# Unread products of the identity in four places of TensorE's queue: a one-core attention and expert kernel

## The reference

```python
q = (layernorm(x) @ Wq + bq)          # (8, 512, 256), 16 heads of 16
k, v = ctx @ Wk + bk, ctx @ Wv + bv
attn = softmax(clip(q @ k.T * 16 ** -0.5, -1e4, 1e4))
x = x + tanh(g_xattn) * ((attn @ v) @ Wo + bo)

xn = layernorm(x)
logits = xn @ gate_weight.T                                # 8 per token
kth = sort(logits.reshape(-1))[4 * 256 * 6 - 1]
gates = logits * (logits >= kth)
h = gelu(xn @ w1[e].T + b1[e])                             # for each expert e
x = x + tanh(g_ffn) * sum_e(gates[..., e] * (h @ w2[e].T + b2[e]))
```

## Time and profile before

| | us |
|---|---|
| median of 3 runs | 2038.12 |
| lowest and highest | 2036.85, 2041.68 |
| the profiled execution | 2045.47 |
| its span, first to last instruction | 2043.7 |
| mean granted clock over the span | 0.968 of 2.4 GHz |

### The profile page before, as it was taken

The page is one execution under the profiler, slowest core; times in us unless marked ns, Lnnn a source line. Parts: engine busy times, 40 slices in busy tenths (PEclk is TensorE's granted clock), DMA queues, the critical chain, the costliest instruction groups (busy, mean ns, idle before and its releaser), DMA issues.

```text
span 2043.7 us, 31038 instructions
## 1 busy us (share of the span) xinstructions
PE 1917.6 (94%) x8916; PEld 1367.7 (67%) x8916; DVE 1339.5 (66%) x2333; ACT 1242.1 (61%) x2076; POOL 161.0 (8%) x334
## 2 busy tenths in 40 slices
PE   7899999999966989999999999999999999999998
PEld 5733333333335767788878878878877887887886
DVE  6688888888617886655755656565565566656555
ACT  4447676776632232576666767676666666767664
POOL 4201011101115440000000000000000000000000
PEclk9969999999968999999999999999999999999999
DMA  7932222222101325224222233322423223332221
GB/s 243 331 106 80 82 74 74 70 78 66 38 31 44 134 102 189 103 84 171 97 104 104 98 120 130 109 104 83 156 109 109 104 83 129 135 109 83 103 103 52
DMA packets 97267, 220.83 MB, mean 108 GB/s; under 512 B 31330, under 2 KB 49508, under 8 KB 87908
## 3 DMA queue, kind: packets, MB, share of 16 engines
q1 hardware_dynamic: 97124, 219.12, 31.2%
HBM read 178.57 MB, written 40.24 MB: 107 GB/s over the span
## 4 chain that ended last, share of the span: by engine, by line
PE 61%; DVE 4%; issue 2%; ACT 1%; POOL 1%; DMA 0%; SPq 0%; DVEq 0%; ACTq 0%
PE ps_y L2107 29%; PE ps_h L2054 26%; PE ps_h L2012 3%; PE ps_y L2026 3%; DVE h_lo L2382 1%; ACT gelu L2270 1%; DVE h_hi L2378 1%; DVE out_T_acc L2459 1%; DVE early L2516 0%; DVE w_pair L2508 0%; SPq L1824 0%; DVE candidate L2421 0%; DMA gates_scratch<-gate 0%; DVE gated L2452 0%; DMA gate<-gates_scratch 0%
## 5 line engine op out<-in xcount | busy, mean ns | idle before, releaser
L2382 DVE TENSOR_TENSOR h_lo<-gelu,h_hi 128x512 fp32r<-128x512 f32 x512 | 360.2, 708 | 407.9 <-ACT h_hi L2273 405.1
L2054 PE MATMUL ps_h<-x_hi,w_pair 128*128 128x512 f32 x1568 | 570.5, 398 | 15.8 <-ACT gelu L2270 8.3
L2270 ACT ACTIVATE gelu<-early,b 128x512 f32<-128x512 f32 x336 | 243.3, 724 | 239.1 <-DVE early L2516 235.6
L2107 PE MATMUL ps_y<-h_hi,w_hi 128*128 128x512 f32 x896 | 355.6, 397 | 3.5 <-DVE h_lo L2382 3.5
L2054 PEld LDWEIGHTS ps_h<-x_hi,w_pair 128*128 128x128 f32 x1568 | 296.1, 189 | 92.9 <-ACT gelu L2270 10.2
L2107 PE MATMUL ps_y<-h_hi,w_lo 128*128 128x512 f32 x896 | 355.1, 396 | 0.0
L2107 PE MATMUL ps_y<-h_lo,w_hi 128*128 128x512 f32 x896 | 354.6, 396 | 0.0
L953 DVE TENSOR_REDUCE low<-ps_s 128x1 f32<-128x512 f32 x512 | 322.2, 684 | 42.8 <-PE ps_s L810 40.8
L2054 PE MATMUL ps_h<-x_lo,w_pair 128*128 128x512 f32 x784 | 310.4, 396 | 0.0
L2273 ACT ACTIVATE h_hi<-gelu 128x512 fp32r<-128x512 f32 x448 | 283.3, 632 | 18.1
L1067 ACT ACTIVATE probs_T<-ps_t 128x512 f32<-128x512 f32 x384 | 207.5, 598 | 109.5 <-PE ps_t L820 107.4
(11 more groups left out here) (247 smaller groups left out, 2164.6 us busy)
## 6 DMA issues: line engine op xcount, KB each, us to landing
x_hi<-blocks_scratch SPq DMA_DIRECT2D x28, 1024.0 KB, 5.1
x_lo<-blocks_scratch SPq DMA_DIRECT2D x28, 1024.0 KB, 8.9
x_hi<-blocks_scratch SPq DMA_DIRECT2D x28, 768.0 KB, 6.8
x_lo<-blocks_scratch SPq DMA_DIRECT2D x28, 768.0 KB, 10.5
gate<-gates_scratch SPq DMA_DIRECT2D x64, 256.0 KB, 3.3
q_st<-q_scratch SPq DMA_DIRECT2D x192, 64.0 KB, 2.3
k_st<-k_scratch SPq DMA_DIRECT2D x192, 64.0 KB, 2.3
k_scratch<-k_hl SPq DMA_DIRECT2D x8, 1024.0 KB, 3.9
```

Source lines behind the costliest of these rows:

```text
L2054: mm = pe.matmul(bank, w[wp], x[xp], start=start and n == 0, stop=n == 2, skip_group_check=not start)
L2107: mm = pe.matmul(ps_y[s][:, d, :], w[:, j, at], h[:, c, :], start=(i == 0 and c < 2 and m == 0), stop=(i == QUADS - 1 and c >= 2 and m == 2))
L2270: act.activation(gelu[:, c % GELUS, :], src, ACT.Gelu_apprx_tanh, bias=b1[p][:, j:j + 1]).then_inc(gelu_done, 1)
L2382: dve.tensor_tensor(h_lo[:, j % RING, :], gelu[:, j % GELUS, :], h_hi[:, j % RING, :].bitcast(F32), ALU.subtract).then_inc(h_ready, 1)
```

## The change

A helper `fill(times, i)` writes `times` products of `ident` with `ident` (128x128, float32, no transpose, no semaphore) into bank `ps_t[i % 3]`. Nobody reads them. It is called in four places of TensorE's queue in `build_attend`: 9 times ahead of the first score product; 3 times after every second of the 32 first score products; in `batch(BATCH)` ahead of seven of the eleven closing units, with the numbers of a table; and 16 times after the product with `fits_sum`, ahead of the block's barrier.

```diff
+FILL_FIRST = 9
+FILL_SCORES = 3
+FILL_LATE = {("out", 3): 4, ("rows", 0): 3, ("y", 0): 2, ("x2T", 0): 4, ("xnT", 0): 20, ("logits", 0): 5, ("pick", 0): 3}
+FILL_END = 16
...
+            def fill(times, i=0):
+
+                for n in range(times):
+                    pe.matmul(ps_t[i % BANKS][:, 0:P], ident[:], ident[:], start=True, stop=True)
...
                 if before:
                     pe.wait_ge(taken[before[0]], before[1] + 1)
+                if isinstance(b, int) and b == BATCH:
+                    fill(FILL_LATE.get((kind, i), 0))
                 write[kind](bank(kind, b + off, i), b + off, i).then_inc(in_psum[kind], 1)
...
+            fill(FILL_FIRST)
             for g in range(2):
                 for t in range(TT):
                     for i in range(GROUP):
                         scores(0, g, t, i)
+                        fill(FILL_SCORES * (i % 2), i)
...
             pe.matmul(ps_m[:, 0:1], ones[:], fits_sum[:], start=True, stop=True).then_inc(fits_in_psum, 1)
+            fill(FILL_END)
```

## The result

The changed kernel takes 2041.68 us (median of 20 runs, 2036.6 to 2046.05) against 2038.35 us (20 runs, 2035.83 to 2042.31) for the kernel before, taken beside it: 1.0015 times as long, with a 95% interval from 1.0008 to 1.0021. That is 3.3 us slower. It is inside the 0.3% that the prediction took for no change, and inside its range, but the sign is the other one: -0.8 us was forecast, and more runs than I had reckoned with make the 3.3 us plain.

What follows compares the result with a forecast made beforehand. Serial pieces, with DVE pacing the first scores and low-clock TensorE on the path elsewhere, were taken as the bound; -0.9 - 0.4 + 0.5 = -0.8 us from 2038.12 gave 2037.3 us, range 2031 to 2043.5.

Steps and rivals of the forecast that it cites:

- The 6.8 us behind the sixteen: Behind the block's closing products: two barriers, branches and the new block, 6.8 us in which TensorE has nothing, taken as unchanged.
- everything behind the experts' start only moves: After the experts' start: the rest of the kernel only shifts with the earlier pieces; +0.5 us added for their first products.
- The first scores and the steps: From the block's start to the fourth `probs_v`: it comes at 138.6 instead of 139.43, -0.9 us.
- no cost: Three products after each pair of scores: TensorE needs 1.19 us against DVE's 1.21, so DVE still sets the pace.
- The fall of the clock among the nine: Ahead of the first score: if the clock falls at 105.4, the delay is +3.5 us and the fourth `probs_v` +0.4 us.
- The closing units: Last batch's chain: filling fits the waits and brings full clock from `rows` on; product with `fits_sum` 4 us earlier.
- The sixteen: Products ahead of the block's closing barrier: 4.0 us on TensorE alone while other engines wait, taking back the closing units' gain.
- (a): Rival at the first scores: clock falls in the first products and stays low; +22 us, 2060 us; 7%.
- (b): Rival at the block's end: the closing sixteen cost nothing, hidden by 6.8 us of barriers and branches; 2033.4 us; 7%.
- (c): Rival at the experts' start: the sixteen carry the clock to the experts; -2.9 us, 2035.2 us; 5%.
- (e): Rival on the price of all filling: a record is cheaper, 0.13 us a product; 2033.4 us; 8%.
- (d): Rival over all low-clock stretches: all low time costs half of itself; 33 us less, 2005 us; 3%.

Runs made afterwards that it cites:

- the third experiment: Only the filling ahead of the last batch's closing units added to the kernel before, the other fillings zero: 2040.27 us, ratio 1.0009.
- the seventh experiment: Only the closing units' filling, plus 23 products in the branch that isn't taken, against the kernel before: 2031.21 us, ratio 0.9964.

## Why the prediction was wrong

- **The 6.8 us behind the sixteen** ("two barriers, the branches and the new block", taken as unchanged) was the step that failed. TensorE's code behind the block lies 456 instructions further on, the reading of the second flag came 3.2 us late, and the 6.97 us of C2 became 13.52 - 3.5 = 10.0 without the sixteen's share. That it is the place of the code was shown both ways: 112 products that never run put 2.0 us into the kernel before, 17 took 3.1 us (13.52 to 10.44) out of the changed one. The trace of before had the kind of stall in it, as 3.95 us at a branch in TensorE's sequencer and 2.9 us of "issue" at the experts' branches, and I took them for fixed. With them fell the sentence that everything behind the experts' start only moves: the waits at their branches depend on the place of the code as well, as the third experiment shows.
- **The first scores and the steps**, forecast at -0.9, were +1.8. Filling products back to back cost 0.125 us a record, as forecast (2.25 us for 18). Between scores six cost 0.86 us and not 0.75 (110.25 to 111.11), so a pair took 1.30 us and passed DVE's 1.21, which "no cost" depended on: 2 x 16 reductions, 0.7 us for each sixteen. The fall of the clock among the nine, which I had as the lesser case, came too, but the trace where it stayed full was only 0.35 us shorter in S. Kernels that left this stretch as it was took 32.8 to 36.1 us in S (six traces, that of before among them; 34.4 in the mean), with low stretches of 23.9 to 34.1 us; the changed opening took 36.1 to 36.5 in three. So 34.67 was no unlucky value, and the loss is about 2 us. (The recorded 138.6 against 139.43 is -0.8, not -0.9.)
- **The closing units** were under-sized: 5.6 us and not 4.0. From `out` to `rows` full clock gave 0.5 us that the sum didn't have, the last product with `clip_flag` 0.2, the four ahead of `out` cost 0.6 and not 0.9, and `y` gave 2.2 and not 1.9; `logits` and `pick` went as worked out. POOL's part stayed: `xnT` still waited for DVE 1.2 us behind the twenty.
- **The sixteen** were right: 3.8 us, all on the path, no help to the experts (0.66 of full clock in their first 6.1 us, had 0.72).
- **The rivals.** (a) did not happen in the changed kernel; without the nine its pace is real, for nine pairs. (b), (c) and (e) fell. (d) fell: in the two profiled executions the low time shrank from 132.6 to 67.9 us, and the median time grew by 3.3, since much of it was beside DVE's work or TensorE's own waits. The rule of the Trainium skill (TensorE: Matmul & The Clock Gate, section Terms), low time multiplied by one minus the granted share, gives an estimate of 32 us for that, and these runs don't agree with it.
- **The range** held the time (2031 to 2043.5), but by luck: two errors of one sign, +3.2 and +2.7, met one of -1.6. Their sum lost the sign.

## What to carry to other kernels

Filling is free only inside waits that are longer than it. Behind a barrier and ahead of one each product was paid in full (2.25 us for nine, 3.8 us for sixteen), and between scores, where the forecast left two hundredths of a microsecond for each pair, the excess was paid sixteen times over. Inside the waits of 0.7 to 5.7 us of the closing chain it brought 4.5 to 5.6 us. Before an edit of some microseconds is judged, look whether it moves code: the same executed instructions took 2040.27 or 2031.21 us here, and the difference between the programs is 92 instructions that never run. An honest comparison of such edits holds the place of the code behind them.

## What the runs showed of the hardware

- TensorE's sequencer stalled 1.8 to 3.2 us in the second flag block in kernels whose code behind lay 164, 192, 448 and 456 instructions further on, and not at 0, 36, 64, 256, 512 and 524. That fits a period of 256 instructions; no run tried other values.
- The traces tell what TensorE waits for there. The page has a DMA queue of instructions (`q8 instruction: 69, 1.13, 0.2%` in the changed kernel: 69 packets, 1.13 MB), whose packets have 16384 bytes each. In most of the experts' part of the kernel before and of the changed one a packet starts on average for every 258 and 250 records of TensorE. Each record that came late began 1.3 to 1.4 us after such a packet had ended (in us; the times of single packets and of the sequencer's records are in the traces, and the views leave them out):

```
kernel                             packet              TensorE goes on
changed                            610.85 to 612.30    613.69
three after each pair, alone       621.55 to 622.52    623.87
closing units alone                606.22 to 607.29    608.62
before, with 112 that never run    613.80 to 614.99    616.36
before, the branch of 3.95 us      614.18 to 615.83    617.20
```

In the kernels without the stall the packet comes too, while the flag is read, and TensorE doesn't wait. The experts' branch waits of 4.5 and 4.4 us have two packets each in them, those of about 3 us in the seventh experiment one. So the stalls are waits for instructions, as closely as times can show it; that a packet of 16384 bytes holds 256 instructions, which would give the period, is worked out from these numbers and not shown by itself.

- A clock that stayed low under a full queue: with three products after each pair alone TensorE was busy 20.76 of 20.80 us, and the grant was low for 20.5 us. In the changed kernel it fell at 105.7 among the eighteen records of the nine and was full again 3.4 us later.
- Six filling records took 0.75 us at the pace of the eighteen and 0.86 us between two scores; four took 0.64 there.
